# A macaron transformer layer on one core: two more tiles' first feed-forwards in iterations 0 and 1, four tiles ahead in place of two, and the weight fit behind a later low part

## The reference

```python
x = x + 0.5 * ffn(layernorm(x))
x = x + attention(layernorm(x))        # 16 heads of 8, softmax over 256 keys;
                                       # inside: layernorm(ctx + x) * gamma + beta
x = x + 0.5 * ffn(layernorm(x))        # the same weights as the first
# ffn: h = concat([h, -h]); h = s0 * (h @ W0); h = 2 * relu(h)
#      h = s1 * (h @ W1); h = 2 * relu(h); s2 * (h @ W2)
#      W0 256x512, W1 512x512, W2 512x128, each entry +1 or -1 from a boolean
```

## Time and profile before

| what | value |
|---|---|
| median of 3 runs | 828.3 us (827.98 to 829.57) |
| profiled execution | 827.32 us, its span 825.5 us |
| TensorE matmul busy | 715.6 us (87%) |
| VectorE busy | 640.2 us (78%) |
| ScalarE busy | 507.7 us (62%) |
| GpSimd busy | 374.5 us (45%) |
| mean granted TensorE clock | 0.964 |

### The profile page before, as it was taken

How to read it: one execution, slowest core, us unless ns; L and a number is a source line. 1 busy time by engine, 2 the same in 40 slices (tenths; PEclk the granted TensorE clock), 3 DMA queues, 4 the chain that set the end, 5 groups by cost and what they waited for, 6 DMA issues and landing times.

```text
span 825.5 us, 18461 instructions
## 1 busy us (share of the span) xinstructions
PE 715.6 (87%) x7258; PEld 330.3 (40%) x7258; DVE 640.2 (78%) x1228; ACT 507.7 (62%) x739; POOL 374.5 (45%) x663
## 2 busy tenths in 40 slices
PE   5668696999999999999999999999999997987767
PEld 2333243444443444444443444444444444342333
DVE  6558678798888989798888879798888877786343
ACT  3325566666666676666766667666667665675632
POOL 4540427355261827255362728264462626254250
PEclk9989698999999999999999999999999999999797
DMA  3011010100101010110101010100101010100000
GB/s 67 24 35 59 2 39 22 40 33 16 46 15 60 14 60 16 40 34 15 46 15 59 15 60 15 54 21 27 46 3 60 15 46 16 46 15 3 14 13 13
DMA packets 29508, 25.62 MB, mean 31 GB/s; under 512 B 4336, under 2 KB 29424, under 8 KB 29424
## 3 DMA queue, kind: packets, MB, share of 16 engines
q1 hardware_dynamic: 28992, 24.07, 9.3%
q10 hardware_dynamic: 432, 0.39, 0.1%
HBM read 5.05 MB, written 4.19 MB: 11 GB/s over the span
## 4 chain that ended last, share of the span: by engine, by line
PE 53%; DVE 29%; POOL 6%; ACT 6%; issue 5%; POOLq 0%; DVEq 0%; ACTq 0%
DVE row_max L1092 12%; PE ps_z L596 11%; PE ps_z L597 10%; PE ps_c L726 9%; DVE ffn_lo L1042 9%; PE ps_s L675 5%; ACT ffn_hi L833 4%; PE ps_m L649 4%; DVE ffn_bn L1019 2%; PE ps_z L580 2%; PE ps_z L586 2%; PE ps_m L738 2%; DVE q_lo L1083 1%; PE ps_m L660 1%; DVE ffn_lo L1045 1%
## 5 line engine op out<-in xcount | busy, mean ns | idle before, releaser
L1092 DVE TENSOR_REDUCE row_max<-ps_s 128x4 f32<-128x1024 f32 x256 | 311.5, 1217 | 37.5 <-PE ps_s L675 35.6
L866 ACT ACTIVATE probs<-ps_t,score_scale 128x1024 f32<-128x1024 f32 x256 | 284.3, 1110 | 76.7 <-PE ps_t L688 76.5
L833 ACT ACTIVATE ffn_hi<-ps_z 128x512 f16<-128x512 f32 x288 | 170.8, 593 | 151.9 <-PE ps_z L597 64.0
L1042 DVE SCALAR_TENSOR_TENSOR ffn_lo<-ps_z,ffn_hi 128x512 f16<-128x512 f32 x256 | 174.0, 684 | 72.3 <-ACT ffn_hi L833 69.0
L596 PE MATMUL ps_z<-ffn_hi,w 128*128 128x512 f16 x512 | 196.2, 383 | 5.3 <-DVE ffn_lo L1042 4.4
L597 PE MATMUL ps_z<-ffn_lo,w 128*128 128x512 f16 x512 | 195.0, 381 | 0.0
L726 PE MATMUL ps_c<-probs,v_cols 128*32 128x256 f32 x2048 | 134.2, 390 | 5.9 <-issue 5.9
L675 PE MATMUL ps_s<-k_rows,q_rows 32*128 32x256 f16 x1024 | 102.8, 279 | 29.9 <-DVE row_max L1092 26.9
L688 PE MATMUL ps_t<-q_rows,k_rows 32*128 32x256 f16 x1024 | 102.9, 280 | 4.6 <-ACT probs L866 4.5
L491 POOL TENSOR_TENSOR max_scaled<-row_max,max_unit 128x16 f32<-128x16 f32 x64 | 14.1, 221 | 168.2 <-DVE row_max L1092 168.2
L596 PEld LDWEIGHTS ps_z<-ffn_hi,w 128*128 128x128 f16 x512 | 49.9, 98 | 85.8 <-DVE ffn_lo L1042 26.0
(11 more groups left out here) (122 smaller groups left out, 968.2 us busy)
## 6 DMA issues: line engine op xcount, KB each, us to landing
x<-L_attn_x SPq DMA_DIRECT2D x16, 256.0 KB, 2.6
q_rows<-q_hi SPq DMA_DIRECT2D x32, 128.0 KB, 2.1
y<-x SPq DMA_DIRECT2D x16, 256.0 KB, 2.1
k_rows<-k_hi SPq DMA_DIRECT2D x30, 128.0 KB, 2.1
q_rows<-q_lo SPq DMA_DIRECT2D x16, 128.0 KB, 2.1
q_rows<-no_max SPq DMA_DIRECT2D x16, 128.0 KB, 2.1
k_rows<-k_lo SPq DMA_DIRECT2D x15, 128.0 KB, 2.1
q_rows<-max_rows SPq DMA_DIRECT2D x64, 8.0 KB
```

The costliest lines, as they stand in the source:

```text
L833: a_.activation(ffn_hi[:, use, :], ps_z[use % 2][:], ACT.Relu if use else ACT.Copy, scale=1.0 if use else XN_SCALE).then_inc(z_hi, 1)
L866: a_.activation(probs[n % PROBS][:, j:j + 2, :], ps_t[:], ACT.Exp, scale=score_scale[:, 0:1]).then_inc(s_exp, 1)
L1042: v.scalar_tensor_tensor(out=ffn_lo[:, use, :], in0=ps_z[use % 2][:], scalar=0.0, in1=ffn_hi[:, use, :], op0=ALU.max, op1=ALU.subtract).th ...
L1092: v.tensor_reduce(row_max[hb % 2][:].rearrange("p (a l) e -> p l a e", a=2)[:, j:j + 2, :, g % 2], ps_s[:].rearrange("p l (a k) -> p l a k ...
```

## The change

- Iterations 0 and 1 each get two first feed-forwards: `ffn_b` in the first half (tiles 2 and 4, from `x0`) and a new `ffn_b2` in the second half (tiles 3 and 5, from `x3`, which is free at that time). SP loads tiles 3 and 5 into `x3` at the top of iterations 0 and 1, behind a wait for the residual of feed-forward 1 or 3.
- From iteration 2 on the first feed-forward is that of tile t+4 in place of t+2. So iterations 12 and 13 have none, and keep the second feed-forward of tile t-2 in their second half. The order of feed-forwards becomes 0 to 5 for tiles 0 to 5, then first and second in turn.
- `x1` has four buffers in place of two.
- Iteration 0 uses the same units as the others: `PACE_ZERO` and `AT_ZERO` go, tile 1's projections stand at units 10 to 31, and its row copies on SP stand where those of the other iterations do.
- The statistics and the norm of tile 2 are taken ahead of iteration 0: the statistics in unit 9 of feed-forward 1, the norm at the end of GpSimd's preparation.
- `setup_fit` moves from behind piece 5 to behind piece 9 of feed-forward 0.

```diff
@@ constants
-PACE_ZERO = {5 + piece: piece for piece in range(15)}
-AT_ZERO = {"LNT": 2, "Q": 4, "K": 6, "V": 8}
+X1S = 4
@@ Iteration
+        self.prep_stats = prep_stats
+        self.ffn_a, self.ffn_b, self.ffn_b2 = ffn_a, ffn_b, ffn_b2
+        self.ffn_late = ffn_a if ffn_b2 is None else ffn_b2
+        self.stats_late = cur and self.ffn_late is not None
@@ order of the work
         def first_ffn(tile):
-            return tile if tile <= 3 else 2 * tile - 4
+            return tile if tile <= 5 else 2 * tile - 6
         def second_ffn(tile):
-            return 2 * tile + 5 if tile <= T - 5 else T + tile
+            return 2 * tile + 7 if tile <= T - 7 else T + tile
+        def b_tile(t):
+            return 2 + 2 * t if t <= 1 else t + 4
+        def x0_loads(tile):
+            return tile // 2 + 1 if tile <= 6 else tile - 2
         def full(t, r):
-            return Iteration(t, r, ffn_a=second_ffn(t - 2), ffn_b=first_ffn(t + 2),
-                             next_b=first_ffn(t + 3) if t + 3 < T else None, misc_base=6 * t + 2)
-        head = [Iteration(0, 0, prev=False, ffn_b=2, next_b=3, misc_base=4, pace=PACE_ZERO),
-                Iteration(1, 1, ffn_b=3, next_b=4, misc_base=8)]
+            first, after = b_tile(t), b_tile(t + 1)
+            return Iteration(t, r, prev=t > 0, ffn_b=first_ffn(first) if first < T else None,
+                             ffn_b2=first_ffn(first + 1) if t <= 1 else None,
+                             ffn_a=second_ffn(t - 2) if t >= 2 else None,
+                             next_b=first_ffn(after) if after < T else None, misc_base=6 * t + 2 if t else 4)
@@ ffn_work
             if 1 <= s < HALF and it.ffn_b is not None:
-                return [(it.ffn_b, False, s - 1)]
-            if s > HALF and it.ffn_a is not None:
-                return [(it.ffn_a, True, s - HALF - 1)]
+                return [(it.ffn_b, s - 1)]
+            if s > HALF and it.ffn_late is not None:
+                return [(it.ffn_late, s - HALF - 1)]
@@ SP, steps
+                if t <= 1:
+                    sp.wait_ge(z_free, Z_USES * (2 * t + 2))
+                    sp.dma_start(x3[:].rearrange("p (b a) d -> p b a d", b=2),
+                                 tile_rows(x_flat, start_of(2 * t + 3))).then_inc(s_odd, 16)
                 if not it.prev:
-                    sp.wait_ge(m_free, it.misc["K"] + 1)
-                    spread(1 - par, 0, SPREADS)
                     place_max(t, par, 0)
                 if it.next_b is not None:
-                    start = start_of(t + 3)
+                    start = start_of(b_tile(t + 1))
@@ GpSimd
             pool.wait_ge(s_norm_in, 16 * 3)
+            ffn_norm(2, x0)
                     att_norm(t + 1, 1 - par)
-                if not it.prev:
-                    ffn_norm(it.ffn_b, x0)
                 if it.cur:
                     tail_base(t, par)
-                if it.stats_a:
-                    ffn_norm(it.ffn_a, x2[par])
+                if it.stats_late:
+                    ffn_norm(it.ffn_late, x3 if it.ffn_a is None else x2[par])
@@ VectorE
+            def residual_b(tile, src):
+                ffn_residual(first_ffn(tile), src, x1[tile % X1S], based=tile - X1S + 1 if tile >= X1S else None)
-                elif s == 5:
+                elif s == 9:
                     setup_fit()
@@ VectorE, feed-forward 1
+                elif s == 9:
+                    dve.wait_ge(s_x0, 16 * 2)
+                    ffn_stats(x0)
+                    ffn_mean_var_wait(2)
+                    ffn_mean_var(2)
             mean_var(att_bn, att_mv, TT, a_mv)
-            dve.wait_ge(s_x0, 16 * 2)
-            ffn_stats(x0)
-            ffn_mean_var_wait(2)
-            ffn_mean_var(2)
@@ VectorE, steps
-                    next_prep = it.ffn_b is not None
+                    next_prep = it.prep_stats
                         ffn_residual(second_ffn(t - 3), x2[1 - par], x3, stored=t - 3)
+                    elif s == 0 and t:
+                        residual_b(b_tile(t - 1) + 1, x3)
-                    if it.stats_a and s == AT_STATS_A:
-                        dve.wait_ge(s_x2, 2 * (t - 1))
-                        ffn_stats(x2[par])
+                    if it.stats_late and s == AT_STATS_A:
+                        if it.ffn_a is None:
+                            dve.wait_ge(s_odd, 16 * (t + 2))
+                            ffn_stats(x3)
+                        else:
+                            dve.wait_ge(s_x2, 2 * (t - 1))
+                            ffn_stats(x2[par])
```

More of the change, by code:

```diff
@@ L87, in __init__ @@
         self.own_contexts = own_contexts
-        self.stats_a = cur and ffn_a is not None
+        self.ffn_late = ffn_a if ffn_b2 is None else ffn_b2
+        self.stats_late = cur and self.ffn_late is not None
         names = [n for n, _ in MISC if
@@ L150, in macaron_layer @@
         x0 = sb("x0", [P, TT, P])
-        x1 = [sb(f"x1_{i}", [P, TT, P]) for i in range(2)]
+        x1 = [sb(f"x1_{i}", [P, TT, P]) for i in range(X1S)]
         x2 = [sb(f"x2_{i}", [P, TT, P]) for i in range(2)]
@@ L263, in macaron_layer @@
         assert LAST_FFN == 2 * T - 1
-        assert (LOOP_TO - LOOP_FROM) % 2 == 0 and LOOP_FROM % 2 == 0
         def run(eng, steps):
-            for it in head:
-                steps(it)
-            for t in range(LOOP_FROM, LOOP_TO):
+            for t in range(T - 2):
                 steps(full(t, t % 2))
@@ L798, in steps @@
                         context(tile, parity, g)
-                    for f, _, piece in ffn_work(it, s):
+                    for f, piece in ffn_work(it, s):
                         ffn_piece(f, piece)
```

57 lines of the change are left out of this document (27 added, 30 removed).

## The result

The changed kernel takes 831.31 us, the median of 6 runs (830.74 to 833.07); the kernel before, on the same chips, 828.73 (6 runs, 827.74 to 829.9). The ratio is 1.0035, with a 95% interval of 1.0022 to 1.0048: slower by 2.9 us (the two medians are 2.6 apart). The forecast was 4.0 more, 832.3. The profiled execution took 830.74 us, with a span of 828.9 and a mean granted clock of 0.958; before it was 827.32, 825.5 and 0.964.

What follows compares the result with a forecast made beforehand. TensorE was taken to bound steady halves, VectorE close behind, with room at the head. Terms from the start to the halves behind the emptied ones summed to +3.98 us, taking the median 828.3 to 832.3; range 829.5 to 835.5.

Steps and rivals of the forecast that it cites:

- The start, -1.24: Before iteration 0: with tile 2's statistics moved away, the first row maximum starts at 53.13 instead of 54.37 us.
- The fit, 0: Feed-forward 0 ends 1.8 us sooner, but feed-forward 1 still waits for GpSimd's normalised input, so the gain is 0.
- Rival 4: At the start: the moved weight fit pays its 1.8 us in full, the rest as forecast, 830.5 us; chance 0.05.
- Iteration 0, -0.13 + 5.08: Halves laid out by hand: first 21.7 us against 21.83, second, now with a feed-forward, 21.4 against 16.32.
- Iteration 1, -2.61 + 7.06: It becomes steady: first half 23.08 us against 25.69, no longer at half clock; second 23.00 against 15.94.
- Iteration 2, -1.54: First half falls to the steady 23.08 us from 24.62, the excess being read as slow clock.
- Iteration 11, -0.54: Second half takes 22.46 us and not 23.00, without statistics for a next first feed-forward.
- The emptied halves, 2 x 20.6: First halves of iterations 12 and 13: GpSimd's split at 11.15, then projections at half clock, 20.6 us against 23.08; -4.96 together.
- Rival 1: Emptied halves stay at full clock, take 18.6 us, and halves behind them pay nothing: 824.9 us; chance 0.15.
- rival 2: Each emptied half takes 15.94 us, like the empty half of iteration 1: 823.0 us in all; chance 0.05.
- The halves behind them, +1.7 each: Second halves of iterations 12 and 13 start at slow clock and take 24.16 us; +1.16 and +1.70, together +2.86.
- Iteration 1's load and the row copies: SP's added wait and load, and the row copies queued behind, delay nothing: 0, with 1 us of slack.

Runs made afterwards that it cites:

- e2: The kernel before with only the weight fit moved, from behind piece 5 to behind piece 9 of feed-forward 0: 827.68 us, ratio 0.9996 to the kernel before.
- e7: The changed kernel with GpSimd's two large memsets moved to right behind its reduction over partitions: 836.98 us, ratio 1.0112 to the kernel before.
- e1: The changed kernel with the weight fit put back behind piece 5 of feed-forward 0: 832.1 us, ratio 1.0057 to the kernel before.
- e9: e8 with 13 more constant matmuls in units 1 to 4 of iteration 0: 819.49 us, ratio 0.9894 to the kernel before.
- e4: The changed kernel with 31 constant matmuls in each emptied first half of iterations 12 and 13: 824.76 us, ratio 0.9967 to the kernel before.
- e6: The change with one feed-forward moved in place of two: only iteration 1's empty half filled, only iteration 13's emptied; 831.71 us, ratio 1.0045 to the kernel before.
- e10: The kernel before with constant matmuls in the empty stretches of iterations 0 (30) and 1 (18): 825.16 us, ratio 0.9962 to the kernel before.
- e11: e10 with GpSimd's last split of tile 1's row maxima ahead of tile 0's second tail norm: 824.7 us, ratio 0.9961 to the kernel before.
- e3: The changed kernel with GpSimd's first split and tail base ahead of the second feed-forward's norm in iterations 12 and 13: 827.57 us, ratio 0.9997 to the kernel before.
- e8: The changed kernel with e3's GpSimd order and 22 constant matmuls in each emptied half: 822.30 us, ratio 0.9933 to the kernel before.
- e12: e9 with 16 more constant matmuls in units 7 and 8 of iteration 14: 817.63 us, ratio 0.9882 to the kernel before.

## Why the prediction was right, and where it wasn't

The sign and the size hold: 2.9 us by the ratio where 4.0 was forecast, inside the forecast's own range. The mechanism holds in the main (filled halves at full price, emptied halves held up by GpSimd's order and half clock), but the head was forecast 2.0 too cheap and the halves behind the emptied ones 2.5 too dear. By its steps:

- *The start, -1.24*: -0.83. The term is smaller than the scatter of this point between runs, 52.6 to 54.5, which the forecast did not have: the clock was 0.83 between 26 and 46 us, and 0.91 before. *The fit, 0*: right by e2's time. Its cover was right too: a gap that nothing of VectorE's sets (e7). Rival 4 falls for the kernel before; in the changed kernel e1's trace speaks against it and its time does not decide.
- *Iteration 0, -0.13 + 5.08*: +1.39 + 4.52, the first mis-sized term. Laid out by hand, the first half came to 21.7 and took 23.22. The chain itself was about right, for at full clock it takes 21.92 (e9), though the 21.7 had one stretch of half clock in it; the clock was half until 63 in place of one stretch, which the forecast had only in its upper end, as +1.3 us. VectorE's wait of 0.35 for tile 3's load is not shown to be part of it: in e1 and e4 there is none, and the half took 23.17 and 23.24. The second half took 20.84 where 21.4 was laid out. e6 shows that 1.7 of iteration 0's growth comes without a second feed-forward there.
- *Iteration 1, -2.61 + 7.06*: -2.30 + 7.07. The 2.61 was clock (e10 gives 2.40), and the first half is 23.39 for 23.08.
- *Iteration 2, -1.54*: -1.55 for its first half, so the number was right and its reason wrong. It was no slow clock (e10), but 0.4 of GpSimd's order and 1.14 of where the cut lies (e11). What made the number right is that a steady half replaced it, whatever the cause; the 1.14 is also part of the +7.07 of the half ahead, so the sum is untouched. The second half, forecast at 0, took 23.28, +0.28.
- *Iteration 11, -0.54*: 22.47 as forecast. The kernel before had 23.36 there and 22.72 in the next half, for its row maximum between them starts 0.36 later behind the scores; the two add up to a steady pair.
- *The emptied halves, 2 x 20.6*: 2 x 21.02, with the split at 11.16 and the clock at half; the chain behind the split took 9.86 where 9.35 was added up. The pieces are shown: order 2.2 to 2.4 and clock 2.3 to 2.5 each (e3, e4, e8). At full clock the forecast had 18.6, and e4 took 18.50. Rival 1 was thus the right price for a case that did not come about; rival 2's, 15.94, is near e8's 16.32, for which GpSimd must be reordered as well.
- *The halves behind them, +1.7 each*: the second mis-sized term, and the step that failed. They paid 0.3 and 0.6. The 1.7 leaned to the 1.54 of iteration 2, which was no clock at all, and 2.61 stood for a half that began with over 4 us of half clock; here it reached 0.6 and 1.1 us into the halves behind. Over the runs this price lies between 0.3 and 1.7 (e3, e6: 1.7), so no single number was to be had before the run. The term is 2.5 too dear, and the emptied halves gave 0.8 less than forecast, which leaves the 1.6 of the table. That and the head's excess of 2.0 are of opposite sign, and that they nearly cancel is luck.
- Iteration 1's load and the row copies cost nothing, as forecast: VectorE's wait for tile 3 in iteration 0 is the only one on an x load in these iterations. The first row maximum of iteration 3 came at 190.36; the forecast's terms add up to 188.4 there, not to the 188.6 that it gave as a sign.

Why a large move of work changed little is then plain. Two feed-forwards cost 5.9 + 4.8 - 1.3 = 9.4 at the head, where empty halves of 16 us become full ones. At the other end they could give 2 x (23.08 - 16.32) = 13.5, and give 4.3, because the emptied halves run into GpSimd's order and a clock that falls. With both mended the change beats both kernels: 0.9933 (e8), and 0.9894 with the clock held at the start too (e9), where constant matmuls in the thin stretches of the kernel before reach 0.9962 (e10). What the kernel before would gain from the same two remedies in its iteration 14 was not run.

## What to carry to other kernels

A stage that loses its heavy work does not shrink to the length that its light neighbour shows elsewhere: ask which engine's order had been hidden behind the heavy work, and what the thin stretch does to TensorE's clock, here some 2.3 us each of a half of 21. Where a thin stretch must stay, constant matmuls in its gaps can hold the clock (31 in each of two halves took 2.5 us out of each), though not surely: the same 13 held it in e9's profile and not in e12's. And before a stage's excess is given a cause, look where its cut lies: a cut at an instruction that is late in one stage and prompt in another moved 1.14 us between two neighbours, and a price read from it was used in the wrong place.

## What the runs showed of the hardware

- GpSimd was idle 5.5 to 6.1 us with nothing to wait for ahead of PARTITION_ALL_REDUCE, and 6.8 to 7.7 us ahead of the first TENSOR_TENSOR behind it, whether that came at once or 4.5 us of memsets later; the memsets themselves ran without a pause.
- The clock fell to half (1.2 GHz) in stretches where TensorE was never idle for long: in e12's iteration 0 its longest wait since 43 us was 0.54 when the clock fell at 62.4, and it was busy for 1.50 and 1.00 us of the two 2 us before. In the changed kernel the falls came after longer waits: at 56.1 after one of 1.86 (busy for 1.00 of the 2 us before), and at 612.5 inside one of 1.33.
- A half clock that reaches into a dense half costs half of its time there (0.3, 0.6 and 1.7 us for a granted clock of 0.93, 0.86 and 0.57 over the first 4 us). In iteration 0, where TensorE also waits for others, 6.8 us of it cost 1.0 to 1.3.
- How soon the clock comes back differs from run to run under the same instructions: the halves behind an emptied one paid 0.3 to 1.7 us. In e12's profile it was also half for a while in iteration 0 (0.72 in 60 to 66 us), though the same constant matmuls had held it in e9's.
